# GpSimd adds the two key halves of the exponentials ahead of the softmax-sum matmul, in a fused gated cross-attention and quantized-MLP kernel on one Trainium2 core

## What is computed

```python
def _mha(query, key, value, Wq, bq, Wk, bk, Wv, bv, Wo, bo):    # 16 heads of 32
    q, k, v = proj(query, Wq, bq), proj(key, Wk, bk), proj(value, Wv, bv)
    scores = jnp.einsum('bhqd,bhkd->bhqk', q, k) / jnp.sqrt(dk)
    p = jax.nn.softmax(scores, axis=-1)                          # 256 keys
    x = jnp.einsum('bhqk,bhkd->bhqd', p, v)
    return jnp.einsum('bsd,ed->bse', x.reshape(B, S, D), Wo) + bo

x = x + jnp.tanh(g_xattn[0]) * _mha(_layernorm(x), ctx, ctx, ...)
xq = _act_fake_quant(_layernorm(x), clip_x)                      # one scale over the whole tensor
h = _act_fake_quant(silu(xq @ Wg.T) * (xq @ Wu.T), clip_down)    # weights fake-quantized by row
x = x + jnp.tanh(g_ffn[0]) * (h @ Wd.T)
```

## Time and profile before

| | |
|---|---|
| median of three runs | 1925.95 us (1925.78 to 1926.21) |
| profiled execution: its span | 1922.0 us |
| one pass of the phase 1 loop | 79.69 us (14 passes) |
| phase 1 ends, phase 2 begins | about 1379 us |
| TensorE, VectorE, ScalarE, GpSimd busy over the span | 91%, 75%, 45%, 26% |

### The profile page before, as it was taken

One profiled execution on the slowest core, in us unless ns is written; L12 is line 12 of the kernel. 1 busy time (PEld: TensorE's weight loads), 2 busy tenths in 40 slices (PEclk: granted clock), 3 DMA queues, 4 the chain that ended last, 5 costly groups with the idle time before them and its releaser, 6 DMA issues.

```text
span 1922.0 us, 36400 instructions
## 1 busy us (share of the span) xinstructions
PE 1748.1 (91%) x12892; PEld 921.0 (48%) x12892; DVE 1443.9 (75%) x1917; ACT 866.1 (45%) x1036; POOL 497.1 (26%) x686
## 2 busy tenths in 40 slices
PE   3999999999999999999999999995599999989787
PEld 3455555555555555555555555543344444434333
DVE  6558778787786877868778687777767877878555
ACT  3243433434335343353442524424777777756242
POOL 5212323223232232322323223202000000006644
PEclk9899999999999999999999999998799999999999
DMA  5422332323323233232332332215225444115897
GB/s 186 110 69 87 87 107 77 105 84 87 109 84 97 87 85 110 85 93 95 84 105 82 93 104 66 73 44 177 109 105 224 186 171 178 45 44 198 339 419 301
DMA packets 132189, 239.73 MB, mean 125 GB/s; under 512 B 17456, under 2 KB 66608, under 8 KB 129584
## 3 DMA queue, kind: packets, MB, share of 16 engines
q1 hardware_dynamic: 132144, 239.14, 37.5%
HBM read 126.10 MB, written 62.39 MB: 98 GB/s over the span
## 4 chain that ended last, share of the span: by engine, by line
issue 37%; PE 35%; DVE 13%; POOL 8%; DMA 4%; ACT 2%; POOLq 0%; DVEq 0%; SPq 0%; ACTq 0%
PE bank L1242 11%; PE bank L1151 6%; PE bank L1153 6%; PE bank L1152 6%; PE spair L1224 4%; DMA x<-out_dram 4%; DVE rs L834 3%; POOL xl L485 3%; POOL yh L559 3%; DVE mx L842 3%; DVE xbuf L806 2%; ACT xh L580 1%; DVE ndev L866 1%; PE spair L1202 1%; DVE parts L821 1%
## 5 line engine op out<-in xcount | busy, mean ns | idle before, releaser
L593 ACT ACTIVATE pr<-spair 128x1024 f32<-128x1024 f32 x256 | 259.2, 1020 | 141.9 <-PE spair L1224 141.9
L842 DVE TENSOR_REDUCE mx<-spair 128x4 f32<-128x1024 f32 x256 | 304.7, 1214 | 0.9 <-PE spair L1202 0.7
L834 DVE RECIPROCAL rs<-bank 128x256 f32<-128x256 f32 x128 | 224.7, 1755 | 58.0 <-PE bank L1242 57.6
L821 DVE SCALAR_TENSOR_TENSOR parts<-bank,bqk,parts 128x512 f16<-128x512 f32 x128 | 94.6, 748 | 135.8 <-ACT parts L586 135.8
L515 POOL TENSOR_TENSOR ol<-o,oh 128x256 f16<-128x256 f32 x128 | 86.4, 675 | 391.7 <-ACT oh L602 382.9
L586 ACT ACTIVATE parts<-bank,bqk 128x512 f16<-128x512 f32 x128 | 88.0, 687 | 215.4 <-PE bank L1153 215.4
L1357 PE MATMUL spair<-xqT,wgT 128*128 128x512 bf16 x704 | 182.3, 382 | 1.3 <-ACT xqT L703 1.3
L1357 PE MATMUL spair<-xqT,wuT 128*128 128x512 bf16 x704 | 181.7, 381 | 0.0
L1202 PE MATMUL spair<-stacks 96*128 96x256 f16 x1024 | 144.4, 279 | 18.2 <-ACT pr L593 10.2
L1242 PE MATMUL bank<-pr,v 128*32 128x256 f32 x2048 | 138.6, 388 | 23.0 <-DVE o L836 23.0
L1224 PE MATMUL spair<-stacks 128*128 128x256 f16 x1024 | 152.5, 275 | 6.3 <-DMA stacks<-mT 6.0
(11 more groups left out here) (172 smaller groups left out, 3422.7 us busy)
## 6 DMA issues: line engine op xcount, KB each, us to landing
stacks<-parts SPq DMA_DIRECT2D x768, 64.0 KB, 2.0
x<-out_dram SPq DMA_DIRECT2D x32, 1024.0 KB, 11.0
h_spill<-hb SPq DMA_DIRECT2D x10, 2816.0 KB, 9.2
hb<-h_spill SPq DMA_DIRECT2D x10, 2816.0 KB, 15.3
xbuf<-in_x_dram SPq DMA_DIRECT2D x16, 1024.0 KB, 5.3
cbuf<-in_ctx_dram SPq DMA_DIRECT2D x16, 1024.0 KB, 5.3
xres<-in_x_dram SPq DMA_DIRECT2D x16, 1024.0 KB, 5.1
out_dram<-xres SPq DMA_DIRECT2D x16, 1024.0 KB, 4.3
```

The source lines that it names most:

```text
L593: act.activation(pr[:, u % 4, :, :, :].rearrange("p a b q -> p (a b q)"), spair[u % 2][:, :, :].rearrange("p a q -> p (a q)"), ACT.Exp, sc ...
L834: dve.reciprocal(rs[:, g % 2, :], obank[:, S:2 * S]).then_inc(recip_done, 1)
L842: dve.tensor_reduce(mx[:, h:h + 2, b, :], spair[u % 2][:, :, :].rearrange("p a (q k) -> p a q k", q=KH), AX_X, ALU.max).then_inc(max_done, 1)
```

## The change

GpSimd gets a new function, `add_halves`. For each unit it adds the two key halves of the exponentials in `pr` into a new buffer `ph`, 128 x 512 f32, with four slots. `pv` issues its value matmuls first (8 calls, as before), then waits for the two added units of its group, then issues the matmuls with `onesP` on `ph`: 4 calls in place of 8. GpSimd's program for a block is rewritten: for each g, two `add_halves`, then `o_low` of the group before, then for g < 4 one tile of `residual` in place of all four at the start, and `x_rstds` at g = 6 in place of g = 3. `o_low(7)` follows the loop. The other engines' programs are as they were.

```diff
+        ph = alloc(p1, "ph", [P, 4, 2, S], F32)
...
+        halves_added = sem("halves_added")
...
-            def residual(j):
+            def add_halves(j, u):
+
+                wait(pool, exp_done, j * NU + u + 1)
+                wait(pool, pv_mm, j * NGR + u // 2 - 1 + 2)
+                pool.tensor_tensor(ph[:, u % 4, :, :], pr[:, u % 4, :, 0, :], pr[:, u % 4, :, 1, :],
+                                   ALU.add).then_inc(halves_added, 1)
+
+            def residual(j, t):
 
                 wait(pool, res_in, j * 16 + 16)
-                for t in range(NT):
-                    pool.tensor_tensor(xres[:, t, :], xres[:, t, :], tgbo[:, :], ALU.add).then_inc(res_bias, 1)
+                pool.tensor_tensor(xres[:, t, :], xres[:, t, :], tgbo[:, :], ALU.add).then_inc(res_bias, 1)
...
             def body(j, nxt):
-                residual(j)
                 for g in range(NGR):
-                    o_low(j, g)
-                    if g == 3 and nxt is not None:
+                    add_halves(j, 2 * g)
+                    add_halves(j, 2 * g + 1)
+                    if g >= 1:
+                        o_low(j, g - 1)
+                    if g < NT:
+                        residual(j, g)
+                    if g == NGR - 2 and nxt is not None:
                         x_rstds(nxt)
+                o_low(j, NGR - 1)
                 if nxt is not None:
                     low_parts(nxt)
                 x1_rstds(j)
...
-                for ones in (False, True):
-                    for kh in range(KH):
-                        for a in range(HPC):
-                            h = HPC * c + a
-                            at = S if ones else 0
-                            last = pe.matmul(obank[DK * a:DK * a + DK, at:at + S],
-                                             onesP[:, :] if ones else v[:, 2 * b + kh, DK * h:DK * h + DK],
-                                             pr[:, (2 * g + a // 2) % 4, a % 2, kh, :],
-                                             start=(kh == 0), stop=(kh == KH - 1))
+                for kh in range(KH):
+                    for a in range(HPC):
+                        h = HPC * c + a
+                        pe.matmul(obank[DK * a:DK * a + DK, 0:S], v[:, 2 * b + kh, DK * h:DK * h + DK],
+                                  pr[:, (2 * g + a // 2) % 4, a % 2, kh, :], start=(kh == 0), stop=(kh == KH - 1))
+                wait(pe, halves_added, j * NU + 2 * g + 2)
+                for a in range(HPC):
+                    last = pe.matmul(obank[DK * a:DK * a + DK, S:2 * S], onesP[:, :],
+                                     ph[:, (2 * g + a // 2) % 4, a % 2, :], start=True, stop=True)
                 last.then_inc(pv_mm, 1)
```

## The result

The changed kernel takes 2525.86 us (median of four runs, 2520.43 to 2527.41) against 1925.87 us for the kernel before on the same chip: a ratio of 1.311 with a 95% interval of 1.309 to 1.313. I had forecast 2512.

The account below looks back on a forecast made before the run. TensorE's instruction stream was taken to set the loop's pace. 1922 us + 382 for the closed chain, the saved 55 included, + 204 for the clock = 2508, with 4 us of median over span 2512; range 2330 to 2690.

Parts of the forecast that it names:

- The main step: Group part: additions wait behind `o_low`, closing a chain once per group; a step takes 9.46 or 8.22 us against 5.44.
- My sum for a pass: One loop pass: 24.9 us later by the chain, plus 13 us for clock drops after six of seven gaps.
- My 599.82: Predicted start of `pv(1)`'s sums, behind residual tile 0: 595.95 + 1.24 + 2.48 + 0.15.
- The six steps from `pv(1)` to `pv(7)`: Sums to sums: three steps of 9.46 us, two of 8.22, and 9.58 to `pv(7)`, at full clock.
- The price of a gap: TensorE after a gap: lowered clock costs 1.7 or 2.65 us of work, mean 2.2; 204 us in all.
- Most of GpSimd's idle time: Phase 1: the wait of `ol` for `oh` was called most of GpSimd's idle, 382.9 us over 119 times.
- adds nothing: Stretched part of a pass: VectorE has idle time there and adds nothing to the time.
- The failed step: Shared port of VectorE and GpSimd: VectorE is near idle while the additions run, so the rule asks for little.
- The signs listed ahead: Changed kernel's pass: `ph` idles of 4.5, 3.2, 5.7 us, `ol` after `oh`, about 118 us, clock 0.75 to 0.85, later phases unchanged.
- The rivals: Whole kernel: clock holds, 2308 (0.11); clock low throughout, 2685 (0.14); dearer additions, 2606; faster, 1871 (0.03); no effect.
- with full clock: Rival for the whole kernel: the chain closes but the clock holds, 1926 + 382 = 2308 us; chance 0.11.
- A price of 1.66 us for an addition: Rival for GpSimd's additions: 1.66 us each, 0.84 us more per step, +94 us, 2606 with the clock term.

Follow-up runs that it names:

- run 4: Changed kernel with GpSimd's order redone: `o_low(g-2)` behind group g's additions, residual tiles at g = 1 to 4, `x_rstds` behind the last additions; 1967.6 us.
- run 3: Changed kernel with extra, unneeded sum matmuls on TensorE filling the gaps before the wait for the added halves; 2348.5 us, 1.220 of the kernel before.
- Run 7: Kernel before, plus two spare GpSimd additions per block on a buffer no other engine touches; 1955.9 us, ratio 1.016.
- the repaired order: Changed kernel with GpSimd's new order in full, 1967.6 us; the same with group 0 keeping its old sums and no additions, 1900.7 us.
- runs 1 and 2: Changed kernel with one order moved: `o_high(g-1)` ahead of `exps(2g+3)` and `qk_high(g+2)` on ScalarE, 2098.3 us; `o_low(g-2)` for `o_low(g-1)` on GpSimd, 2080.7 us.
- the filled run: Changed kernel with its TensorE gaps filled by extra sum matmuls that the real ones overwrite; 2348.5 us, ratio 1.220 to the kernel before.
- run 8: Kernel before with all 16 additions per block spare, on a buffer no other engine touches, and GpSimd in its new order; 1974.3 us, ratio 1.025.

## Why the prediction was right

**The main step held.** The chain from `qk` through `qk_high`, `o_high`, `o_low` and the additions to the sums closes once per group. Cut at either of two places, it gives back 428 and 445 of the 600 us. The order in which engines wait decided it, not the amount of work: GpSimd does all 256 additions in run 4 too.

**The pass, term by term.** My sum for a pass was 24.9 us of chain and 13 of clock, 37.9; measured are 119.47 - 79.69 = 39.8.
- Start to the sums of `pv(1)`: GpSimd's first addition stands at 820.12, its small steps end at 819.82 (588.51 before), an offset of 231.31. My 599.82 becomes 831.13; the sums of `pv(1)` came at 833.09. 1.96 late: `ndev` is 1.91 us longer, and the reload of `xres` waits for it. **Not in my sum.**
- The six steps from `pv(1)` to `pv(7)`: 63.55 us, summed 54.40, and 53.92 at full clock in run 3. So the clock took 9.6 here, and my chain was 0.5 too long.
- From the sums of `pv(7)` to `xl`: 918.97 - 896.64 = 22.33 us, before 647.88 - 628.86 = 19.02, less 0.43 for the halved sums. 3.7 us more. The first `vproj` runs at the lower clock, 902.59 - 897.66 = 4.93 in place of 632.46 - 629.86 = 2.60: 2.3. About 1.4 is left, and VectorE's first layer norm tile takes 2.25 us in place of some 0.53 there, since it now falls behind GpSimd's `cl`.

Together 24.9 + 2.0 + 9.6 - 0.5 + 2.3 + 1.4 = 39.7. The clock comes to 11.9 us a pass, where I had 13.

That the total came within 14 us of 2526 is in part luck. I had left out 3.4 us a pass, and 1.6 that I had too much hid half of it. The price of a gap was a mean of two rows; the single gaps here cost between 0 and 2.8 us.

**Two readings that were wrong.** "Most of GpSimd's idle time" goes to the wait for `oh`: in a block it is 382.9 / 16 = 24 us, and GpSimd is idle for 79.69 - 23.39 = 56, so it is the largest part and not most. And VectorE "adds nothing": it adds the 2.0 and the 1.4 us. The first changes nothing in the sum.

**The failed step** is the sentence "VectorE is near idle while the additions run here, so this rule asks for little". The rule of the Trainium skill (SBUF — State Buffer, Who interferes with whom) is that a GpSimd operation and a VectorE operation in a two-port mode lock each other out of a shared port. The runs agree that the two delay each other: `ndev`, a `tensor_scalar` from SBUF to SBUF, went from 1.92 to 3.83 and 4.83 us. The port and the mode themselves no trace here shows. VectorE isn't idle when group 0's additions run; it is computing `ndev`, with `norm(0)` queued behind. For the later groups the sentence holds in the changed kernel: there VectorE waits while the additions run. Run 7 isolates the price, 29 us with nothing else changed, its share of the clock included. I had looked at what VectorE would do to the additions, and not at what they would do to it. The trace of before had the sign for it: a tile of the layer norm that took 1.27 us while `cl` ran on GpSimd (634.65 to 638.87), and 0.53 or 0.54 us in the three other tiles of that pass:

```profile
637.87 1.27 DVE L806 TENSOR_SCALAR xbuf<-xbuf,mv,rstd 128x512 f32<-128x512 f32 x1
```

In the changed kernel this is small beside 600 us, so the forecast survived. In the repaired order it decides the sign: 1968 against 1901 us. It is also part of the miss of runs 1 and 2, whose expectations left it out.

**The signs listed ahead.** `ph` idle 4.1 to 4.3 and 2.9 us (summed 4.45, 3.21), 4.21 before `pv(7)` (summed 5.7; there TensorE's part was longer at the lower clock). The pass 119.5, not 118. The clock 0.77 in the group part (0.75 to 0.85). Phases 2 and 3 as before. The rivals: with full clock the time would have been 2308, and the filled run at 2348 shows that state, apart from its own waits. A price of 1.66 us for an addition was wrong: the mean is 1.281.

**Open.** TensorE's unnamed waits in run 3 were not tested. Why equal gaps cost 2.8 and 1.7 us of clock stays open too. The clock's part behind `pv(7)`, 2.3 us a pass, is read from one pass of the changed kernel, not from a run that changes the clock alone.

## What to carry to other kernels

When work moves to an idle engine, read its program as a queue: list each wait that stands ahead of the new work, and follow it until it either ends early or comes back to the engine that you wanted to relieve. Here an engine busy for 26% of the time made the kernel 31% slower by waiting in the wrong place; one wait placed a group later gave back three quarters of it. Then look at what the second engine runs at that very moment: leaving out the additions of one group in eight, those beside `ndev`, turned a 2% loss into a gain. A gap on TensorE can be paid twice; its second price, the clock, was 9.6 us in six steps here, and the length of a single gap didn't tell it.

## What the runs showed of the hardware

- VectorE's f32 `tensor_scalar` from SBUF to SBUF and GpSimd's `tensor_tensor` delay each other, also for tiny operands: 128x4 elements took 0.61 and 1.19 us in place of 0.17. So does a `scalar_tensor_tensor` on 128x4 elements: `shift` took 0.99 us in place of 0.15 (run 8). Reciprocals that read PSUM weren't touched (1.75 us in all runs).
- Extra matmuls can save time: 177 us here, with clock 1.00 in the filled stretch against 0.77. The stretch itself shrank from 63.55 to 53.92 us.
- GpSimd's 128x512 f32 addition takes 1.24 us back to back with two different inputs; with the same operand twice and in place, two took 2.04 us.
